# A Mamba, cross-attention and mixture-of-experts block: softplus in one table function, a fourth product on GpSimd, and a last batch worked in halves

## The reference

```
x_ssm, z = split(x @ W_in.T)                  # 512 channels each
x_ssm = silu(causal_conv4(x_ssm) + conv_b)
B, C, r = x_ssm @ W_x.T                       # 16 states each, and one column
dt = softplus(r * W_dt + b_dt);  A = -exp(A_log)      # A: 512 x 16
h[t] = exp(dt[t] * A) * h[t-1] + (x_ssm[t] * dt[t]) * B[t]    # per channel and state
y = sum over states (h * C) + x_ssm * D_param;  y = (y * silu(z)) @ W_out.T
```

## Time and profile before

| what | value |
|---|---|
| time, median of 3 | 1605.9 us |
| profiled execution: its own time | 1608.83 us |
| profiled execution: span of the core | 1607.0 us |
| mean granted PE clock | 0.941 of full speed |
| DVE busy | 1395.5 us, 87% |
| PE busy | 1336.6 us, 83% |
| ACT busy | 1120.9 us, 70% |
| POOL busy | 997.6 us, 62% |

### The profile page before, as it was taken

One profiled execution on the slowest core, in us unless ns is written; L12 is line 12 of the kernel. 1 busy time (PEld: TensorE's weight loads), 2 busy tenths in 40 slices (PEclk: granted clock), 3 DMA queues, 4 the chain that ended last, 5 costly groups with the idle time before them and its releaser, 6 DMA issues. The chain is left out here.

```text
span 1607.0 us, 22613 instructions
## 1 busy us (share of the span) xinstructions
PE 1336.6 (83%) x7516; PEld 935.6 (58%) x7516; DVE 1395.5 (87%) x2549; ACT 1120.9 (70%) x2566; POOL 997.6 (62%) x688
## 2 busy tenths in 40 slices
PE   6787778778778777787786989999999999999796
PEld 4566667656656666676665653547354735473375
DVE  5899999999999999999999862678888887888785
ACT  5878888897798888888878624336833783377464
POOL 2899999999999999999998711100740083018101
PEclk9988999999999999998998987999999999999898
DMA  6102211220221022112102004100001001000000
GB/s 211 70 1 71 83 38 47 83 71 15 83 83 64 20 84 83 40 45 83 65 14 102 14 14 165 57 1 1 1 27 57 1 1 37 17 1 0 27 1 27
DMA packets 44599, 76.43 MB, mean 48 GB/s; under 512 B 3841, under 2 KB 38242, under 8 KB 40258
## 3 DMA queue, kind: packets, MB, share of 16 engines
q1 hardware_dynamic: 44482, 74.98, 13.4%
HBM read 66.06 MB, written 8.91 MB: 47 GB/s over the span
## 5 line engine op out<-in xcount | busy, mean ns | idle before, releaser
L977 POOL TENSOR_TENSOR state_c<-state,c_area 128x1024 f32<-128x1024 f32 x256 | 600.3, 2360 | 34.6 <-DVE state L1054 31.3
L1054 DVE TENSOR_TENSOR_SCAN state<-decay,ps 128x512 f32<-128x512 f32 x416 | 503.3, 1212 | 10.5 <-ACT decay L731 9.0
L731 ACT ACTIVATE decay<-step_area,negA 128x255 f32<-128x255 f32 x832 | 351.6, 497 | 0.5 <-DVE step_area L1132 0.5
L1754 POOL TENSOR_TENSOR big<-big,g_sb 128x1024 f32<-128x1024 f32 x26 | 68.2, 2622 | 389.1 <-ACT big L1622 378.1
L1022 DVE TENSOR_TENSOR ps<-step_area,ps 128x512 f32<-128x512 f32 x416 | 283.6, 682 | 12.3 <-PE ps L410 9.9
L426 PE MATMUL ps<-ident_sb,state_c 128*128 128x128 f32 x2048 | 283.0, 286 | 1.6 <-DVE yg L1008 0.9
L426 PEld LDWEIGHTS ps<-ident_sb,state_c 128*128 128x128 f32 x2048 | 252.3, 149 | 28.1 <-issue 14.3
L946 POOL TENSOR_TENSOR ub<-step_area,b_bc 128x1024 f32<-128x1024 f32 x48 | 113.3, 2360 | 27.9 <-DVE step_area L1135 27.9
L1554 PE MATMUL ps<-w_sb,hT 128*128 128x256 f32 x512 | 119.4, 385 | 6.2 <-ACT ps L1646 3.8
L410 PE MATMUL ps<-parts,sel_bc_sb 96*128 96x256 bf16 x208 | 61.5, 296 | 72.8 <-DVE ps L1038 60.5
L1054 DVE TENSOR_TENSOR_SCAN state<-ps,ub 128x512 f32<-128x512 f32 x96 | 116.1, 1209 | 6.8 <-ACT ps L744 5.7
(11 more groups left out here) (235 smaller groups left out, 2565.5 us busy)
## 6 DMA issues: line engine op xcount, KB each, us to landing
c_area<-bc_scratch SPq DMA_DIRECT2D x32, 1024.0 KB, 8.0
b_bc<-bc_scratch SPq DMA_DIRECT2D x16, 384.0 KB, 4.8
weights<-in_xT SPq DMA_DIRECT2D x16, 256.0 KB, 3.1
res<-in_x SPq DMA_DIRECT2D x16, 256.0 KB, 2.8
x_scratch<-res SPq DMA_DIRECT2D x16, 256.0 KB, 2.1
weights<-x_scratch SPq DMA_DIRECT2D x4, 1024.0 KB, 9.0
xa<-x_scratch SPq DMA_DIRECT2D x4, 1024.0 KB, 5.6
out_x<-acc SPq DMA_DIRECT2D x3, 1024.0 KB, 4.4
```

The source lines that it names most:

```text
L731: nc.scalar.activation(decay_tile(i, n)[:, j, 1:], dt_sb[:, i[1] % 2, j, 1:], ACT.Exp, scale=negA[:, j * NS + n:j * NS + n + 1]).then_inc( ...
L977: nc.gpsimd.tensor_tensor(state_c[:, n % RING, :, :], state[:, n % RING, :, :], c_bc[:, q, n, :].unsqueeze(1).to_broadcast([P, CT, TC]), A ...
L1054: nc.vector.tensor_tensor_scan(state[:, n % RING, pair, :].rearrange("p j n -> p (j n)"), a, b, 0.0, ALU.mult, ALU.add).then_inc(s_scan, 1)
```

## The change

It has four parts.

**1. Softplus.** In the turns, `terms` calls ACT's Softplus directly, with a table load before the four instructions and one behind; Abs, Relu, Exp and Ln go, and with them `make_dt` on POOL. The Silus move from slot 10 to slot 9.

**2. Four states on the other path.** `OFF` becomes (2, 6, 10, 14). POOL's products stand in slots 2, 6, 10 and 14. DVE forms two fewer u*B halves and adds two fewer carries per chunk.

**3. Start-up.** PE runs ten matmuls of ones before the weights are there. Channel groups 2 and 3 of chunk 0 are convolved on DVE, groups 0 and 1 on PE. Softplus replaces the long way here too, u is made in halves, and the first gate's copies go behind ACT's first decays.

**4. The last batch and the tail.** The first norm is made for 4 tiles and then for the other 4 (`join`, `finish`). PE fills the gap with two matmuls, transposes the first half, starts the first expert layer with it, and transposes the second half after three tiles. The gate, the final norm of batch b-1 and the gate's weights move behind. POOL's last work of batch b-1 waits until all 8 tiles of the last batch are normalised. 12 of the 32 bias instructions go behind the weights of tiles 0 to 3. In the tail, POOL takes three tiles (0, 1, 3), the first terms of the sums go ahead of the wait for the others, and ACT makes its guess before it weighs tile 3.

```
-        OFF, APART = (2, 5, 8), 3
+        WARM = 10
+        OFF, APART = (2, 6, 10, 14), 4
...
+            for _ in range(WARM):
+                nc.tensor.matmul(w_ps[:, 0:P], ones[0:1, :], ones[0:1, :], start=True, stop=True)
...
             def terms(k, j):
                 if j == 0:
+                    nc.scalar.preload_act_table_set("softplus")
                     act.wait_ge(s_step, at(k, 1, 1))
-                nc.scalar.activation(dt_sb[:, k[1] % 2, j, :], w_ps[:, 0:TC], ACT.Abs,
-                                     scale=col("W_dt", j), bias=col("b_dt", j)).then_inc(s_abs, 1)
-                nc.scalar.activation(relu[:, j, :], w_ps[:, 0:TC], ACT.Relu,
-                                     scale=col("W_dt", j), bias=col("b_dt", j)).then_inc(s_abs, 1)
-
-            def softplus(k):
...
+                nc.scalar.activation(dt_sb[:, k[1] % 2, j, :], w_ps[:, 0:TC], ACT.Softplus,
+                                     scale=col("W_dt", j), bias=col("b_dt", j)).then_inc(s_dt, 1)
+                if j == CT - 1:
+                    nc.scalar.preload_act_table_set("natural_log_exp_and_others")
...
-                             (10, lambda: silus(k)), (11, lambda: copies(k)),
+                             (9, lambda: silus(k)), (11, lambda: copies(k)),
...
-                    work += [(9, lambda: split(k, 0)), (11, lambda: make_dt(k)), (11, lambda: first_arg(k)),
+                    work += [(9, lambda: split(k, 0)), (11, lambda: first_arg(k)),
...
-                work += [(1, lambda: product_b(i, OFF[1])), (4, lambda: product_b(i, OFF[2]))]
+                work += [(2, lambda: product_b(i, OFF[1])), (6, lambda: product_b(i, OFF[2])), (10, lambda: product_b(i, OFF[3]))]
...
+            for j in range(2, CT):
+                src, done = xi[:, j, HALO:HALO + TC], TAPS * (j - 2)
+                nc.vector.tensor_scalar(xs[:, 0, j, :], src, col("conv_w", j, TAPS - 1), col("conv_b", j),
+                                        ALU.mult, ALU.add).then_inc(s_cv, 1)
+                for back in range(1, TAPS):
+                    dve.wait_ge(s_cv, done + back)
+                    nc.vector.scalar_tensor_tensor(out=xs[:, 0, j, back:], in0=src[:, 0:TC - back],
...
-        POOLED = 2
-        ORDER = [0, 1, TT - 1] + list(range(POOLED, TT - 1))
+        POOL_TILES = (0, 1, 3)
+        TAIL_TILES = (2, TT - 1, 4, 5, 6)
+        ORDER = [0, 1, 2, 3, TT - 1, 4, 5, 6]
...
+                    for t in range(TG):
+                        join(t)
+                    aggregate(b, 0, slice(0, TG))
+                    newton(b, 0, slice(0, TG))
+                    for t in range(TG):
+                        finish(t)
+                    for t in range(TG, TT):
+                        join(t)
...
-                        pool.wait_ge(s_x2, (b + 1) * TT + 1)
+                        pool.wait_ge(s_x2, (b + 1) * TT + (TT if b + 1 == LAST else 1))
...
+                    if t == 2:
+                        pe.wait_ge(s_l2c, b * TT + TT)
+                        for late in ORDER[2:]:
+                            first_term(late)
```

More of the change, by code:

```diff
@@ L818, in turn @@
                     step(i, n)
+                    if n == 0 and is_first(i):
+                        first_gate()
                     for place, what in work:
@@ L821, in turn, with first_gate @@
                             what()
+            def first_gate():
+                for t, src in ((0, w_ps[:, :]), (1, y_ps[:, DI:2 * DI])):
+                    act.wait_ge(s_in, CTT + t + 1)
+                    nc.scalar.activation(gate[:, 0, t, :], src, ACT.Copy).then_inc(s_zc, 1)
             act.sem_inc(s_scan, RING * 2)
@@ L1338, in _, with transposes @@
         def _(pe):
-            def transposes(src, bank, done):
-                for u in range(NL * KT):
+            def transposes(src, bank, done, units=range(NL * KT)):
+                for u in units:
                     half, k = u // KT, u % KT
@@ L1504, in gate @@
                     last.then_inc(s_gate, 1)
-                pe.wait_ge(s_x2, b * TT + TT)
-                transposes(xt, 0, s_yt)
-                pe.wait_ge(s_ytc, b * TRB + TRB)
                 if more:
+                    pe.wait_ge(s_x2, b * TT + TT)
+                    transposes(xt, 0, s_yt)
+                    pe.wait_ge(s_ytc, b * TRB + TRB)
                     pe.wait_ge(s_qc, (b + 1) * U + U)
-                gate()
-                for t in range(TT):
+                    gate()
+                else:
+                    pe.wait_ge(s_r, b * TT + TG)
+                    for bank in range(2, 4):
+                        last = nc.tensor.matmul(ps[:, bank, :], ident_sb[:, :], w1_sb[:, 0, 0:HALF], start=True, stop=True)
+                    last.then_inc(s_fill, 1)
+                    pe.wait_ge(s_x2, b * TT + TG)
+                    transposes(xt, 0, s_yt, range(KT))
+                    pe.wait_ge(s_ytc, b * TRB + KT)
+                for t in range(TT):
+                    if not more and t == TG - 1:
+                        pe.wait_ge(s_x2, b * TT + TT)
+                        transposes(xt, 2, s_yt, range(KT, NL * KT))
+                    if not more and t == TG:
+                        pe.wait_ge(s_ytc, b * TRB + TRB)
+                        gate()
                     pe.wait_ge(s_pre, b * 2 * TT + t + 1)
                     for h in range(2):
-                        dst = ps[:, 2 * (t % 2) + h, :]
+                        dst = ps[:, work_bank(b, t) + h, :]
                         for k in range(KT):
@@ L1581, in _, with copy_transposed @@
         def _(act):
-            def copy_transposed(b, dst, bank, ready, done):
-                for u in range(NL * KT):
+            def copy_transposed(b, dst, bank, ready, done, units=range(NL * KT)):
+                for u in units:
                     half, k = u // KT, u % KT
@@ L1714, in turn @@
                             preset(TT + t + 2)
+                        if t == 1 and not more:
+                            gate_exp(b)
                         if t == TG and more:
@@ L1748, in turn @@
                     residual(b + 1)
-                for t in range(TT if more else POOLED):
+                for t in range(TT) if more else POOL_TILES:
                     tile = big[:, t // TG, t % TG, :]
@@ L2018, in turn @@
                     final_aggregate(b - 1)
-                gate_scores(b)
-                if tail:
+                if more and tail:
+                    finished()
+                if more:
+                    gate_scores(b)
+                if more and tail:
                     final_newton(b - 1)
@@ L2052, in turn @@
                 measure(b, 1, TG - 1, s_l1c)
-                aggregate(b, 2)
-                newton(b, 2)
+                aggregate(b, 2 + b // LAST)
+                if not more:
+                    final_newton(b - 1)
+                    final(b - 1)
+                    gate_ranks(b)
+                newton(b, 2 + b // LAST)
                 for i in range(TG):
```

263 lines of the change are left out of this document (144 added, 119 removed).

## The result

The changed kernel takes 1564.96 us (median of 4 runs, 1561.08 to 1568.01) beside 1608.13 for the kernel before on the same chip: the ratio of the runs is 0.9731, with a 95% interval of 0.970 to 0.9762. The forecast was 1559. The profiled execution took 1564.17, its span 1562.4, which is 44.6 less than the span before (1607.0).

What follows compares the result with a forecast made beforehand. DVE bound Mamba with POOL close behind, PE mostly from 923 us on, and the start-up was a chain without overlap. Gains of 22 (Mamba), 9 (start-up) and 16 (last batch), 47 us, from the median 1605.9 gave 1559; range 1547 to 1583.

Steps and rivals of the forecast that it cites:

- The convolution's share: Start-up: PE convolves half the groups, 3.5 us less; DVE's eight instructions finish about 0.7 us behind PE's half.
- The chain behind the last Silu: Start-up, last Silu to first scan: loads, projection and step, Softplus, decays 6.4 us, plus 0.3 for hand-overs; was 10.9.
- If the ten matmuls bring PE to the quick pace beforehand: Start-up: the in-projection's 16 entries then take 3.5 us in place of 5.66, 2.1 less, at worst nothing.
- its lower bound: Start-up: gain of only 5 us, without quicker matmuls and with slow hand-overs; forecast 9, at best 10.
- DVE's own work falls to 53.36: Mamba turn: two half steps become scans, taken as 1.15 us less from DVE's 54.51.
- The path becomes 53.99 us, longer than DVE's. POOL is the new bound: Mamba turn: POOL's 53.69 us loses make_dt (2.35) and gains a product with carry (2.65); turn taken as 54.2.
- what is late next is u from POOL: Mamba turn: once ACT's stall at slot 13 goes, u from POOL, needed by DVE in slot 15, is late next.
- The decay wait of slot 13: Mamba turn: DVE's largest idle piece, 0.75 us for a decay of ACT, was to disappear.
- Mamba's 22: Mamba: 1.4 us less per turn over 16 turns gives 22 us; bounds 5 lost and 26 gained.
- The lower end of the range, 1547: Whole kernel: fastest total time, 1547 us, said to come from both upper bounds of Mamba and the start-up.
- 1.5 forecast: Last batch: about 1.5 us given back, as moments of tiles 0 to 3 end later and ACT waits before an eviction.
- The step on POOL's block: Tail: POOL's third tile blocking DVE adds up to 2.3 us, counted as 1.5, leaving a gain of 6.

Runs made afterwards that it cites:

- c1_oldsp: The changed kernel with Abs, Relu, Exp, Ln on ScalarE and make_dt on GpSimd again in every turn, four indices kept: 1595.44 us, ratio 0.9918 to the kernel before.

## Why the prediction was right, step by step

**Start-up.** Forecast 9 us by the first scan, measured 6.75. The convolution's share (PE 3.5 less, DVE finishing 0.7 behind) is confirmed at 2.8. The chain behind the last Silu was put at 6.4 + 0.3 and is 23.43 - 16.66 = 6.8. The step that failed is "If the ten matmuls bring PE to the quick pace beforehand": they bring nothing, 2.1 us are missing, and with full rows they are there. The prediction had this case in its lower bound.

**Mamba, the turn.** The size was wrong and the mechanism half so. "DVE's own work falls to 53.36": in a like turn it is 53.16. I read one ordinary turn of before for all; over 14 turns DVE had 54.17 of work and 1.55 idle, not 54.51 and 1.08, and the first turn of each of the four sequences, which has no carries to add, has less of both engines' work. The step that failed is "The path becomes 53.99 us, longer than DVE's. POOL is the new bound". From one split of B and C (`rest`) on POOL to the next, less its waits, it is 53.5 to 53.9 in three turns of four and 52.4 to 52.6 in the first of a sequence, 53.4 in the mean. That is 0.2 less than forecast in an ordinary turn and 0.6 less in the mean. And POOL does not bound alone: 1.23 us more for DVE cost 1.1, 0.74 more for POOL about 0.3, and about half a us less for POOL gained nothing. The step to "what is late next is u from POOL" failed too. In the 14 turns of the changed kernel DVE never has a listed wait for POOL; it waits for ACT's decays of index 14, 0.63 or 0.64 us in four turns, and 1.02 in the three that have no carries. So the turn is 52.9 to 54.5, with 57.1 in the last but one, and not 54.2, and 14 turns gave 27.6 us, not 19.6. That Softplus is what lets the fourth index pay was in the argument (make_dt gone against a product come), and c1_oldsp shows it. The decay wait of slot 13 is gone; four Softplus take 1.93 us, as four Abs at their pitch of 0.45 would, and the next instruction is 1.30 behind a load, as forecast. The Trainium skill ("ScalarE: Activation LUTs", section "What ACT_TABLE_LOAD costs") has a drain of about 1380 ns beside the load's 1283 at every switch. The trace does not show the drain: the decay ahead of the load ends at 380.21, the load starts at 380.22, and the first Softplus 1.30 behind it.

**Mamba, the last turn.** Nothing in the prediction covers it. I multiplied the gain of a steady turn by sixteen, this one included, and did not look at the one turn in which ACT's slots 10 and 11 hold queries. The stretch from `yg` 15 to attention lost 6.2 us. Split by the runs: with Softplus and three indices it is 4.7 shorter than before, the fourth index adds 10.9, of which the order of slot 10, with the second query's place, is 3.4. About 3.1 more is PE's clock in the stretch ahead of attention (below), and not the index. The other 4.5 are not followed to one cause. Over the whole program the fourth index is worth 8 us by the medians, 1572.5 against 1564 to 1565, and about 12 by the stretches of the profiled executions (3.7 + 16.3 - 7.9), without the 6 us that the clock gave the one with three.

So Mamba's 22 came out as 27.6 less 6.2, and 2.2 more in turn 0 (8.92 by `yg` 1, less the 6.75 of the start-up), which makes 23.6. The 22 is right by luck: two errors of opposite sign, a turn that was forecast too long and a last turn that was not looked at. The lower end of the range, 1547, does not follow from the terms that it names: the upper bounds of Mamba and the start-up with 16 for the last batch give 1554.

**The last batch.** Forecast 16, measured 14.3. First expert layer 11.0 earlier against the join, measured 10.2; start of the second layer 11.4, measured 9.3. What is missing by then is PE's clock, which the sum left out. Windows of 4 us of the changed kernel, then a window and PE's row of the one with less work for GpSimd, which has the same stage:

```profile
1458.00:1462.00 4.00, 1.81 (x9) 1.35 (x8) 3.55 (x13) 1.82 (x3) 0.33 (x1) 0.84 0.00 0
1462.00:1466.00 4.00, 3.31 (x6) 1.51 (x5) 3.25 (x17) 2.05 (x5) 0.00 (x0) 0.50 0.00 0
```
```profile
1460.00:1464.00 4.00, 3.86 (x9) 1.82 (x10) 3.25 (x17) 1.65 (x5) 0.00 (x0) 1.00 0.00 0
```
```profile
1460.14 10.57 PE L1549 MATMUL ps<-w_sb,weights 128*128 128x512 f32 x24 [0.74 <-ACT weights L1626]
```

In the first, the granted clock falls to 0.50 (1.2 GHz) while PE transposes the first half, behind its wait of 2.19 us for DVE. The transposes take 1.75 us instead of 1.09, and the 24 entries 12.86 instead of 10.57. With the clock up the first expert layer is 10.8 earlier than before against the join, and the second 12.2. From the join to the end it is 109.68 us in one and 106.74 in the other. Of the twelve executions with this order of the stage, ten took 109.6 to 109.8 and two 106.7, so the change is worth 14.3 us here as a rule, and 17.2 where the clock stays up. From the start of the second layer to its last matmul 1.7 us were given back (40.0 where it was 38.3), for 1.5 forecast: PE waits 1.44 for ACT's copies, and 1.26 at 1527.77 for ACT, which had waited 2.54 for DVE's numbers behind the moments (at 1525.28). The tail: forecast 6, and from the last matmul of the second layer (1534.94) to the last sum's moments it is 18.1 where it was 24.8.

The step on POOL's block was right in size and wrong in price. Four normalisations took 3.51 us beside POOL's product and 1.38 alone. The Trainium skill ("SBUF — State Buffer", section "Who interferes with whom") states that DVE in a mode that uses both ports and GpSimd block each other for a whole instruction, and these rows agree. PE had sums of other tiles in hand, and the 1.5 us I counted cost nothing.

## What to carry to other kernels

Price the one turn that is not like the others by itself: an order that is tuned for the steady turn can put an instruction behind a wait that only the last turn has. When two engines run within 1% of each other, busy time does not name the bound, and one turn is not all turns; one added instruction on each engine, and one taken away, shows how far each is from the path. Where two edits touch two near bounds, expect each alone to give little, and judge them together.

## What the runs showed of the hardware that was not expected

TensorE's granted clock differs between executions of one kernel, through short drops, and with it the time. The same turn of the same kernel in two executions (the changed kernel, first and second):

```profile
622.41:676.86 54.45, 43.22 (x246) 35.37 (x245) 52.78 (x78) 45.10 (x123) 53.66 (x37) 0.91 0.18 64
```
```profile
622.62:675.58 52.96, 41.91 (x249) 34.37 (x248) 52.74 (x78) 45.85 (x124) 52.17 (x36) 0.94 0.21 66
```

DVE has the same work, 52.8. In the long turn it waits twice:

```profile
658.67 1.22 DVE L1053 TENSOR_TENSOR_SCAN state<-ps,ub 128x512 f32<-128x512 f32 x1 [0.63 <-ACT ps L738]
676.86 1.23 DVE L1005 TENSOR_TENSOR yg<-ps,gate 128x1024 f32<-128x1024 f32 x1 [0.93 <-issue]
```

In windows of 4 us the long turn has the clock below 1.00 from 646.5 to 658.5 and again from 670.5, the short one only from 654.5 to 662.5. The place of a drop decides what it costs. In the first 13 turns of two executions of the changed kernel, the clock was about 0.50 from 24 to 28 us behind `yg` in six ordinary turns (without those that have no carries); in each of the six ACT waited 0.71 or 0.72 us for PE's transposes, and DVE then 0.63 or 0.64 for the decays of index 14. In a seventh, the long turn above, the clock fell inside this stretch (0.75), with the same two waits. Where it stayed at 1.00 from 24 to 31 us, the trace lists neither wait. The drop of the short turn, which lies later, costs nothing. Over nine executions of the changed kernel the times follow the mean clock roughly: spans of 1557.5 at 0.944 and 0.945, 1562.0 and 1562.1 at 0.940, 1566.2 at 0.937, but also 1559.3 at 0.941 and 1564.0 at 0.942. From the last `yg` to the first transpose of attention it shows directly (the changed kernel, and the one with less work for GpSimd):

```profile
902.64:953.85 51.21, 39.51 (x318) 24.50 (x322) 25.32 (x19) 12.18 (x23) 6.08 (x10) 0.70 0.27 96
```
```profile
903.60:951.74 48.14, 36.11 (x318) 22.41 (x322) 25.24 (x19) 12.47 (x25) 5.67 (x7) 0.79 0.26 95
```

The same 318 entries of PE in 3.1 us less. It is one of the two executions that were also 3.0 us shorter in the last batch. What makes the drops fall here or there was not tried. It is why 3 us of real gain in one stretch can vanish in another.
